# Fourier-mode mixing kernel: four channel blocks per step on 32 partitions each instead of two on 64

## What is computed

```python
xs = rfft2(x, axes=(1, 2)).reshape(B, H, W // 2 + 1, 8, 48)          # 33 wave numbers along W, 64 along H
o1r = relu(xr @ w1[0] - xi @ w1[1] + b1[0])                          # per block of 48 channels
o1i = relu(xi @ w1[0] + xr @ w1[1] + b1[1])
o2r = o1r @ w2[0] - o1i @ w2[1] + b2[0]
o2i = o1i @ w2[0] + o1r @ w2[1] + b2[1]
out = irfft2(softshrink(o2r, 0.01) + 1j * softshrink(o2i, 0.01)) + x
```

## Time and profile before

| | |
|---|---|
| three runs | 990.94, 992.49, 998.67 us |
| span of the profiled execution | 991.3 us |
| TensorE busy | 916.0 us, 92% |
| VectorE busy | 577.1 us, 58% |
| ScalarE busy | 475.8 us, 48% |
| DMA moved | 184.41 MB, 186 GB/s over the span |

### The profile page before, as it was taken

The page is one execution under the profiler, slowest core; times in us unless marked ns, Lnnn a source line. Parts: engine busy times, 40 slices in busy tenths (PEclk is TensorE's granted clock), DMA queues, the critical chain, the costliest instruction groups (busy, mean ns, idle before and its releaser), DMA issues.

```text
span 991.3 us, 14302 instructions
## 1 busy us (share of the span) xinstructions
PE 916.0 (92%) x5168; PEld 460.3 (46%) x5168; DVE 577.1 (58%) x869; ACT 475.8 (48%) x757; POOL 81.1 (8%) x157
## 2 busy tenths in 40 slices
PE   2799999999999988999999999999999999999933
PEld 1555555665676655444444434444444444444411
DVE  1255555455454765787775676666666666666511
ACT  2455444444545424434343445565655656666521
POOL 3011111011111110000000101000000000000001
PEclk8899999999999999999999999999999999999986
DMA  9879699469648979856143443343654474554463
GB/s 283 324 206 298 202 282 366 150 180 283 248 136 269 260 237 277 210 138 164 48 114 95 112 127 108 108 123 113 213 170 129 153 247 134 161 156 153 142 192 128
DMA packets 95703, 184.41 MB, mean 186 GB/s; under 512 B 13007, under 2 KB 73769, under 8 KB 93842
## 3 DMA queue, kind: packets, MB, share of 16 engines
q1 hardware_dynamic: 85490, 143.65, 48.0%
q0 software_dynamic: 9696, 39.56, 12.4%
q10 hardware_dynamic: 448, 0.30, 0.1%
HBM read 104.32 MB, written 79.14 MB: 185 GB/s over the span
## 4 chain that ended last, share of the span: by engine, by line
PE 82%; DMA 9%; SPq 2%; DVE 2%; ACT 2%; issue 1%; POOL 0%; ACTq 0%; DVEq 0%
PE psum L948 17%; PE psum L957 16%; PE psum L987 8%; PE psum L1041 6%; PE psum L1065 6%; PE psum L1025 6%; DMA RG<-rows_along_h 6%; PE psum L936 5%; PE psum L967 5%; PE psum L998 4%; PE psum L1052 3%; PE psum L913 3%; PE psum L1014 2%; DMA rows_along_h<-RD 1%; SPq L611 1%
## 5 line engine op out<-in xcount | busy, mean ns | idle before, releaser
L1374 DVE SCALAR_TENSOR_TENSOR RA<-psum,RA 112x896 f32<-112x896 f32 (+1 forms) x120 | 124.1, 1035 | 206.3 <-ACT RA L1222 205.9
L1222 ACT ACTIVATE RA<-psum,small 112x896 f32<-112x896 f32 (+1 forms) x120 | 115.7, 964 | 94.7 <-PE psum L957 94.7
L957 PE MATMUL psum<-RA,RW 112*64 112x448 f32 (+1 forms) x640 | 131.1, 531 | 1.4 <-ACT RA L1213 1.4
L1213 ACT ACTIVATE RA<-psum,RW 112x448 f32<-112x448 f32 (+1 forms) x160 | 89.2, 609 | 80.0 <-PE psum L948 80.0
L1334 DVE COPY RD<-psum 128x672 f32<-128x672 f32 (+2 forms) x122 | 69.5, 571 | 58.3 <-PE psum L987 56.8
L987 PE MATMUL psum<-RD,const 128*128 128x384 f32 (+1 forms) x304 | 98.3, 445 | 3.7 <-DVE RD L1334 2.7
L1207 ACT ACTIVATE RA<-psum 128x384 f32<-128x384 f32 (+2 forms) x72 | 50.6, 702 | 78.9 <-PE psum L936 52.6
L936 PE MATMUL psum<-const,RX 128*112 128x128 f32 x528 | 68.5, 282 | 17.1 <-DMA RX<-rows_along_w 17.1
L1359 DVE TENSOR_TENSOR RX<-RX,RA 112x768 f32<-112x768 f32 (+2 forms) x80 | 80.8, 1011 | 2.5
L1207 ACT ACTIVATE RD<-psum 128x384 f32<-128x384 f32 (+2 forms) x122 | 64.0, 525 | 32.9 <-PE psum L987 30.9
L936 PEld LDWEIGHTS psum<-const,RX 128*112 128x112 f32 x528 | 61.2, 180 | 35.7 <-issue 34.9
(11 more groups left out here) (103 smaller groups left out, 1070.1 us busy)
## 6 DMA issues: line engine op xcount, KB each, us to landing
RG<-rows_along_h SPq DMA_DIRECT2D x7, 3072.0 KB, 11.5
RX<-x SPq DMA_DIRECT2D x16, 768.0 KB, 8.6
rows_along_w<-RX SPq DMA_DIRECT2D x54, 224.0 KB, 5.1
rows_along_h<-RD SPq DMA_DIRECT2D x84, 144.0 KB, 3.3
rows_along_h<-RD SPq DMA_DIRECT2D x56, 168.0 KB, 2.9
out<-RA POOLq DMA_DIRECT2D x12, 768.0 KB, 4.0
RX<-rows_along_w SPq DMA_DIRECT2D x12, 672.0 KB, 6.5
spectrum<-RA POOLq DMA_DIRECT2D x48, 168.0 KB, 4.7
```

The costliest lines, as they stand in the source:

```text
L957: mm = nc.tensor.matmul(bank[b * HALF:(b + 1) * HALF, a * BANK:a * BANK + nk * H], w4[layer][0:ROWS, g, b, a], hidden(slot)[0:ROWS, b * N: ...
L1213: done = nc.scalar.activation(hidden(slot)[0:ROWS, b * N:b * N + nk * H], banks(key)[0:ROWS, b, 0:nk * H], ACT.Relu, bias=bias[layer][0:RO ...
L1222: nc.scalar.activation(dst, src, ACT.Relu, bias=minus_lambda_l0 if key[0] == "S4" else minus_lambda).then_inc(act_emptied, 1)
L1374: nc.vector.scalar_tensor_tensor(out=dst, in0=src, scalar=LAMBDA / 64 if key[0] == "S4" else LAMBDA, in1=dst, op0=ALU.add, op1=ALU.min).th ...
```

## The change

A step now takes four channel blocks, the whole half of 192 channels, so there are 20 steps per layer in place of 40 (`QUADS`). Each block has 32 partitions. The 48 real and 48 imaginary channels of a block are cut into three chunks of 32: 32 real ones, the rest (16 real and 16 imaginary), 32 imaginary ones. A step's modes are thus 128 partitions by three times 448 (or 384) columns.

- `mix_first` makes 12 matmuls, three chunks for each of four row tiles of 32 rows; every block has a PSUM bank of its own. `mix_second` makes 12 matmuls of 112 rows by 32 columns of weights, in four column tiles.
- `S2` makes one matmul of 128 columns of weights per wave number for the 32 first channels of each block and four of 32 columns for the rest. The rest's imaginary half comes out on the wrong partitions and is moved: ScalarE copies it to SBUF and then issues four small DMAs from SBUF to SBUF (`moved_rest`); `S3` waits for them (`wait_rest_moved`).
- Transposes go by pairs of wave numbers, all 128 partitions at a time; `5A` and `5C` contract real and imaginary parts in two matmuls of 64 rows each, in two row tiles. The copies of `TA` and `TC` are split: two chunks on ScalarE, the third on VectorE in two copies.
- The relu of the first product stays on ScalarE, four ACTIVATEs per step. `above`, `shrink`, `add_to` and `join` go over three chunks at once.
- PSUM is no longer four fixed units. `Plan` hands out banks in turn: four for `S2`, `S3`, `3L2`, `3L3`; three for `S4`, `4L2`, `4L3`, `TA`, `TC`; two for the others. TensorE waits for the last owners of just these banks.
- `order()` is written anew with one round per step of four blocks: `S1`, `6A`, `6C` come in runs of four or two; layer 3 runs one step behind layer 2 (before, two of the smaller ones). The spectrum in DRAM is laid out by half and part; `fwd_c` is loaded late, after the last `S4`, since it has lost its own place in SBUF.

```diff
@@ Plan
-    VECTOR = {"PR", "TA"}
-    SCALAR = {"S2", "S3", "H1", "3L2", "3L3", "TC"}
+    VECTOR = {"PR"}
+    SCALAR = {"S2", "S3", "H1", "3L2", "3L3"}
+    BANKS = {"S2": 4, "S3": 4, "3L2": 4, "3L3": 4, "S4": 3, "4L2": 3, "4L3": 3, "TA": 3, "TC": 3}
+    BY_BANK = {"S3", "3L2", "3L3"}
...
+            n = self.BANKS.get(key[0], 2)
+            if at + n > ALL_BANKS and key[0] not in self.BY_BANK:
+                at = 0
+            self.banks[key] = [(at + i) % ALL_BANKS for i in range(n)]
+            at = (at + n) % ALL_BANKS
+            self.before[key] = sorted({owner[b] for b in self.banks[key] if b in owner}, key=self.unit.get)
@@ take
-                at = plan.unit[key]
-                if at >= UNITS:
-                    wait_emptied(pe, plan.order[at - UNITS])
-                return unit(key)
+                for before in plan.before[key]:
+                    wait_emptied(pe, before)
@@ s2
-                for k in range(nk):
-                    at, of = (max(k - 1, 0), k + 1 if k < 2 else 0) if k0 == 0 else (k, 0)
-                    mm = nc.tensor.matmul(bank[0:ROWS, k * P:(k + 1) * P], Bm(e)[:, at, cols], dft_h[:, of * P:(of + 1) * P],
-                                          start=True, stop=True)
+                for k, (at, of) in enumerate(columns):
+                    nc.tensor.matmul(bank[:, k * P:(k + 1) * P], Bm(s)[:, at, PASS_B * REST:],
+                                     dft_h[:, of * P:(of + 1) * P], start=True, stop=True)
+                for k, (at, of) in enumerate(columns):
+                    to = 2 * BANK + k * P
+                    for b in range(PASS_B):
+                        mm = nc.tensor.matmul(bank[b * CHUNK:(b + 1) * CHUNK, to:to + P],
+                                              Bm(s)[:, at, b * REST:b * REST + CHUNK],
+                                              dft_h[:, of * P:(of + 1) * P], start=True, stop=True)
@@ mix_first
-                for a in range(2):
-                    for b in range(2):
-                        rows = slice(b * HALF, b * HALF + BS)
-                        dst = bank[0:ROWS, b * BANK:b * BANK + nk * H].rearrange("p (k h) -> p k h", h=H)
-                        mm = nc.tensor.matmul(dst, w3[layer][rows, a, g], src[rows, :, a], start=a == 0, stop=a == 1)
+                for j in range(CHUNKS):
+                    for b in range(PASS_B):
+                        rows = slice(b * CHUNK, (b + 1) * CHUNK)
+                        mm = nc.tensor.matmul(to[b][0:ROWS, 0:n], w3[layer][rows, half, j], by_chunk(src)[rows, j],
+                                              start=j == 0, stop=j == CHUNKS - 1)
@@ mix_second
-                for a in range(2):
-                    for b in range(2):
-                        mm = nc.tensor.matmul(bank[b * HALF:(b + 1) * HALF, a * BANK:a * BANK + nk * H],
-                                              w4[layer][0:ROWS, g, b, a],
+                for j in range(CHUNKS):
+                    for b in range(PASS_B):
+                        mm = nc.tensor.matmul(bank[b * CHUNK:(b + 1) * CHUNK, j * BANK:j * BANK + n],
+                                              w4[layer][0:ROWS, PASS_B * half + b, j], hidden(slot)[:, b, 0:n],
@@ scalar, stage S2
+                    copy(*rest_views(s)).then_inc(rest_copied, 1)
+                    copy(*main_views(s)).then_inc(act_emptied, 1)
+                    act.wait_ge(rest_copied, s + 1)
+                    for b in range(PASS_B):
+                        dst, src = moved_rest(s, b)
+                        act.dma_start(dst, src).then_inc(rest_moved[s % A_SLOTS], 16)
@@ order, phase C
+        if r < QUADS:
+            o += [("3L2", r)]
+        if 0 <= r - 1 < QUADS:
+            o += [("3L3", r - 1)]
...
+        if 0 <= r - 3 < QUADS:
+            o += [("5C", r - 3, 0), ("5C", r - 3, 1)]
+        if r < QUADS:
+            o += [("4L2", r)]
+        if 0 <= r - 1 < QUADS:
+            o += [("4L3", r - 1)]
         for p in range(PASSES - 1):
...
+            if 0 <= r - last_inverse_round(p) < S1_UNITS // 2:
+                o += [("6C", p, 2 * (r - last_inverse_round(p)) + v) for v in range(2)]
+        if 0 <= r - 2 < QUADS:
+            o += [("TC", r - 2)]
```

More of the change, by code:

```diff
@@ L938, in s2 @@
[L938 to L948 removed]
+                wait_bm_loaded(pe, s)
@@ new lines, in s5 @@
+                d = D(first + e)
+                at = 0
+                if e % PASS_GROUPS == 0 and part == 0:
+                    for a in range(2):
+                        nc.tensor.matmul(bank[:, 0:PASS_C], matrices[2 + a], d[:, 0, a],
+                                         start=a == 0, stop=a == 1)
+                    at = PASS_C
+                for a in range(2):
+                    for half in range(2):
+                        ms = [m for m in bank_columns(e, part, half)[1] if not (at and m == 0)]
+                        rows = slice(half * HALF, (half + 1) * HALF)
+                        to = half * BANK + at * (half == 0)
+                        dst = bank[:, to:to + len(ms) * PASS_C].rearrange("p (k c) -> p k c", c=PASS_C)
+                        mm = nc.tensor.matmul(dst, matrices[a][rows], d[rows, ms[0]:ms[-1] + 1, a],
+                                              start=a == 0, stop=a == 1)
```

815 lines of the change are left out of this document (423 added, 392 removed).

## The result

The changed kernel takes 1066.6 us (median of 4 runs, 1065.3 to 1070.4), the kernel before 995.6 us beside it (990.9 to 1000.7). The ratio is 1.072, its 95% interval 1.067 to 1.077: slower by 7%, where I had forecast 986 us and a range up to 1035.

The account below looks back on a forecast made before the run. TensorE bounded the old kernel; afterwards the engines emptying PSUM would set each round, so most of its 106 us saving would be lost. 991.3 - 10 (A) - 5 + 2 (C) + 9 - 2 = 985, plus 1.2: 986 us, range 945 to 1035.

Parts of the forecast that it names:

- TensorE's work: Both products with four tiles at once: first 2.44 us, second 2.40 us per 448-column step; some 106 us less work in all.
- Rival 2: Slower: four column tiles in second products and `S2` miss full rate; 1125 us, middle case 1030; chance 0.12.
- Phase C: Rounds without `6C` gain 0.65 us in each of 8, 5 us; 12 rounds with `6C`, 18.2 us each, lose 2 us.
- The chain of VectorE: Phase C: VectorE's four operations in a row behind TensorE's 10.2 us set the round's end, 16.4 us against 14.1 of work.
- The Trainium skill's rule: Tiling speeds TensorE but not emptying PSUM; by it the 106 us saved on TensorE would be lost in whole.
- Phase A, plain rounds: Rounds without `S1` or `6A`: mean 12.8 us against 13.2 before, 4 us gained over 10 rounds.
- The issues: Phase A: ScalarE's four DMA issues per step take 1.5 us, with 1.84 us as upper bound.
- Phase A, once each: One-off costs: 3 us layer 3's first product, 3 us sums and `fwd_c`, 3 us first moved rest; 2 us less for a load.
- and `fwd_c` comes late: 3 more: Phase A: layer 1's sums in one VectorE round needed by `6A`, together with the late `fwd_c`, cost 3 us more.
- in six with `6A` ... all but 0.5 us is hidden: Phase A: in six rounds `6A`'s work is hidden but for 0.5 us; 17.8 against 18.8 us, 6 us gained.
- The moved rest at the start: Phase A: the first step's moved rest has no cover yet and costs 3 us once.
- Rival 3: Slower: TensorE idles in rounds with `6C` and its clock falls, up to 1.7 us, 12 to 20 times; 1006 to 1020; chance 0.10.

Follow-up runs that it names:

- c_order: Changed kernel with, in phase C, VectorE doing both shrinks and the copies of `6C` and of the transposes' rest before both adds: 1042.0 us, ratio 1.047.
- five edits of order in A: Changed kernel with `fwd_c` split and loaded earlier, prepared weights stored earlier, third pass's `6A` later, two layer 1 sum loads at round 18: 1026.4 us, ratio 1.031.
- combo5: Changed kernel with five phase A order edits and phase C's adds last, layer 1's three sum loads issued singly at rounds 14, 18, 17: 988.1 us, ratio 0.993.
- y_early: Changed kernel with SyncE issuing the first two loads for layer 1's sums at the top of phase A's round 18: 1073.0 us, ratio 1.080.

## Why the prediction was wrong

- **TensorE's work.** Right: 105 us less, forecast 106. A first product of 448 columns takes 2.3 to 2.5 us (2.44 forecast), a second 2.39 (2.40), so four tiles run at full rate. (By rows 3 and 4, 0.22 us in four record times is 0.385 us for a record of 448 columns and not 0.373: the sum should have said 2.47.) Rival 2 is out, and so is what the Trainium skill's table "Measured speedup vs the span model" in TensorE: Matmul & The Clock Gate would have made of it; the trace differs from it.
- **Phase C.** Right in size, to 1 us (412.2 forecast by its terms, 412.9). The chain of VectorE was right in kind: c_order, which takes the adds out of it, gives 27 us. The exact size is luck. In the eight rounds with `6C` ahead of the last the mean was 19.3 us, not 18.2, with the clock at 1.2 GHz in parts of them: 9 us too many. Against that stand the two waits for transposed loads of 2.5 and 2.3 us that the kernel before has in this phase (the earlier trace rows shows the first) and the changed one has not; the rest of the balance I have not taken apart. And the round without `6C` owes its length as much to ScalarE's `above` of layer 3 as to VectorE's add.
- **The Trainium skill's rule** under "PSUM Bottleneck" of TensorEngine Tiling (Array Packing), that tiling does not speed the emptying of PSUM, is borne out in phase C: 72 us of TensorE's work gone, the phase 3 us longer.
- **Phase A, plain rounds.** Right where the clock stayed up: 12.2 to 13.7 us, forecast 12.8. The issues were mis-sized (2.44 against 1.5 us, above the bound), which cost nothing in these rounds.
- **Phase A, once each.** Here the forecast failed, 328 us by its terms against 402.5. Of the 74 us 32 are clock and some 42 idle time that the walk did not have. The step was "and `fwd_c` comes late: 3 more". I had seen that the load moved behind the last second product and took it for a short one; it was a wait of 20.6 us, for a transfer of 97 rows. No row of before showed it, since nothing waited for it, but the trace of before has it: issued at 161.7, its 97 packets ran one behind the other until 191.0, long before `CF` at 362.3. The rule quoted above would have told me; I had not looked the load's rows up against it. And "in six with `6A` ... all but 0.5 us is hidden" took its input for landed: round 10 took 32.1 us and round 15 23.5, for 17.8 walked (rounds 11 and 16, with 22.6 and 18.6, are as long as the same steps before). The moved rest at the start was mis-sized too, a wait of 5.8 us for 3. I had walked TensorE, ScalarE and VectorE, and not the queues of GpSimd and SyncE, where the store of the weights stands behind a whole step's update and the loads for layer 1 behind the transposed load. The wait before `6A` in the earlier trace rows was for VectorE; I carried that over as the one that counts.
- **What the edits give back.** The five edits of order in A take the profiled A from 402.5 to 357.3 us and the median to 1026.4, half of the way to the forecast; the other 29 us of A above its terms stay open. Round 7, which also has the product for the prepared weights, is among them: 25.2 us in the changed kernel and in combo5, 16.5 walked. That combo5 comes to 988 us, next to the forecast of 986, confirms nothing: a third of its gain is c_order, which the walk did not have.
- **The clock.** Rival 3, with a chance of 0.10 and a place in phase C, was as large an error as the waits: busy time at 1.2 GHz rose from 12 to 104 us, 46 us lost, 32 of them in phase A, a good part of it behind the waits named. It ran with the rest and not beside it: the one wait of which a run gives the price by itself cost half as much again (13.7 for 9.0). Since the first row showed just that, it belonged into the price of every wait, not into a case of its own.
- **The range.** Its upper end, 1035, came from rival 2. The errors of phase A, the late loads and the clock behind them, had one sign, and none of the cases held them.

## What to carry to other kernels

When a step is made wider, walk every in-order queue that carries one-off work too, stores and loads on the queue engines above all: whatever stands behind "one step" now waits for a step twice as long. Price an idle time of TensorE of several microseconds with the clock behind it. And on the engine that empties PSUM, put what frees banks ahead of what only updates SBUF: the same instructions in that order were worth 27 us here.

## What the runs showed of the hardware

- One load of 97 rows of 4096 B took 20.9 us to land, its packets one behind the other; the same data as 96 rows and 1 row took 5.6 us, with up to 19 packets at once.
- Four DMA issues of ScalarE took 2.44 to 2.56 us in most rounds, and up to 9.09 us in others, where the DMA engines were busy and GpSimd issued stores too. An engine that issues DMAs beside its own work can be held for that long.
- Needless matmuls in idle time kept the clock up: with 23 us of them in phase C the busy time at 1.2 GHz fell from 30.3 to 16.1 us, and the kernel got no faster. That every idle time of some length lowers the clock is not shown: combo5 has one of 3.3 us that ends at 152.5 with no fall behind it, and one of 3.4 us that ends at 77.9 with one.
- An edit's gain depended on its company: y_early cost 6 us alone and gave 8 beside the four others. I have not separated how much of that is clock.
